# Half 1's tail into the latent attention, four masks onto POOL, ScalarE's early copies in other places of the scan

## What is computed

```python
# layer 1, first part (L1_attn): a state of 16 x 256 per batch
x_proj = x @ proj_in_w.T + proj_in_b
delta = softplus(x_proj @ B_w.T)                 # 16 step sizes per token
h = h * sigmoid(A) + x_t[:, :, None] * d_t[:, None, :]   # for t in 0..255
y_t = h.sum(axis=1) @ C_w.T + D_param * x_t
out = y @ proj_out_w.T + proj_out_b + x
# layer 1, second part (L1_xattn): 16 heads, keys and values from ctx
kv_c = kv @ W_kvc ; q_c = q @ W_dq               # 64 and 96 wide
scores = (q_nope @ k_nope.T + rope(q_rope) @ rope(k_rope).T) * scale
good = (k_ids <= qs) & (k_ids >= qs - 8)         # a window around seg_id
out = softmax(where(good, scores, -1e30)) @ v @ W_o
```

## Time and profile before

| | us |
|---|---|
| three timed runs | 761.4, 765.0, 765.1 (median 765.0) |
| profiled execution, whole | 760.8 |
| its span, first to last instruction | 759.0 |
| mean granted TensorE clock | 0.971 of full |
| busy in the span: PE, DVE, ACT, POOL | 689.7, 478.9, 319.7, 327.4 |

### The profile page before, as it was taken

One profiled execution on the slowest core, in us unless ns is written; L12 is line 12 of the kernel. 1 busy time (PEld: TensorE's weight loads), 2 busy tenths in 40 slices (PEclk: granted clock), 3 DMA queues, 4 the chain that ended last, 5 costly groups with the idle time before them and its releaser, 6 DMA issues.

```text
span 759.0 us, 12500 instructions
## 1 busy us (share of the span) xinstructions
PE 689.7 (91%) x4578; PEld 535.5 (71%) x4578; DVE 478.9 (63%) x995; ACT 319.7 (42%) x764; POOL 327.4 (43%) x475
## 2 busy tenths in 40 slices
PE   6999799999999888777999999999969999999993
PEld 5766564786576556545778777878848888888883
DVE  5488673331144589976998989872365656565656
ACT  4655533102213866533777677770132222222220
POOL 4323316310101869612866666651244445444521
PEclk9999999998999999998999999999969999999998
DMA  7000015000002000000000000003010211121001
GB/s 262 1 3 2 2 47 231 1 31 19 1 1 79 2 17 1 2 1 0 1 1 2 2 1 1 1 2 104 0 43 22 62 43 42 42 63 43 1 1 55
DMA packets 10462, 23.42 MB, mean 31 GB/s; under 512 B 2082, under 2 KB 5091, under 8 KB 10019
## 3 DMA queue, kind: packets, MB, share of 16 engines
q1 hardware_dynamic: 10402, 22.63, 9.0%
HBM read 21.58 MB, written 1.05 MB: 30 GB/s over the span
## 4 chain that ended last, share of the span: by engine, by line
PE 76%; DVE 15%; ACT 5%; issue 3%; DMA 1%; POOL 0%; POOLq 0%; DVEq 0%; SPq 0%; ACTq 0%
PE psum L399 30%; PE psum L432 8%; PE psum L934 6%; PE psum L965 4%; PE psum L651 4%; PE psum L943 3%; PE psum L455 3%; DVE A L1296 3%; DVE psum L1283 2%; PE psum L734 2%; PE psum L506 2%; PE psum L548 1%; DVE probs L1123 1%; DVE A L1190 1%; PE psum L779 1%
## 5 line engine op out<-in xcount | busy, mean ns | idle before, releaser
L399 PE MATMUL psum<-parts 128*128 128x256 f32 (+2 forms) x1440 | 254.2, 335 | 13.0 <-DVE parts L1144 7.5
L399 PEld LDWEIGHTS psum<-parts 128*128 128x128 f32 (+1 forms) x1440 | 220.5, 193 | 43.6 <-DVE parts L1144 7.5
L1764 POOL TENSOR_SCALAR probs<-probs,row_rec 128x256 f32<-128x256 f32 x128 | 60.6, 486 | 54.7 <-DVE row_rec L1134 53.9
L1474 ACT ACTIVATE probs<-probs,neg_max 128x256 f32<-128x256 f32 x128 | 64.0, 503 | 40.1 <-DVE neg_max L1127 40.1
L1714 ACT ACTIVATE A<-psum 128x512 f32<-128x512 f32 x44 | 26.3, 598 | 129.4 <-PE psum L399 129.4
L1883 POOL CAST parts<-C 128x512 fp32r<-128x512 f32 (+1 forms) x44 | 31.1, 706 | 101.9 <-PE psum L399 91.4
L1421 DVE TENSOR_TENSOR A<-A,psum 128x512 f32<-128x512 f32 x44 | 30.2, 687 | 70.1 <-PE psum L399 70.1
L934 PE MATMUL psum<-C,A 128*128 128x256 f32 x256 | 68.4, 391 | 0.0
L1884 POOL TENSOR_TENSOR parts<-C,parts 128x512 fp32r<-128x512 f32 (+1 forms) x44 | 54.9, 1248 | 3.5
L934 PEld LDWEIGHTS psum<-C,A 128*128 128x128 f32 x256 | 43.8, 190 | 15.1 <-issue 10.5
L1123 DVE TENSOR_TENSOR probs<-psum,ctxT 128x512 f32<-128x512 f32 x64 | 43.6, 681 | 15.5 <-PE psum L934 15.3
(11 more groups left out here) (215 smaller groups left out, 1243.2 us busy)
## 6 DMA issues: line engine op xcount, KB each, us to landing
C<-in_experts SPq DMA_DIRECT2D x22, 384.0 KB, 3.0
A<-in_w_o SPq DMA_DIRECT2D x1, 2048.0 KB, 12.2
x_tok<-in_x_tok SPq DMA_DIRECT2D x1, 1024.0 KB, 7.3
ctxT<-in_ctxT SPq DMA_DIRECT2D x1, 1024.0 KB, 11.0
out<-x_tok SPq DMA_DIRECT2D x8, 128.0 KB, 1.8
A<-in_w_uqT SPq DMA_DIRECT2D x1, 768.0 KB, 6.0
xT<-in_xT SPq DMA_DIRECT2D x2, 256.0 KB, 4.1
C<-in_wqk SPq DMA_DIRECT2D x1, 512.0 KB, 4.6
```

Of the source, the lines that this page charges most:

```text
L399: ins = mm(o, left[l], right[r], start=first and n == 0, stop=last and n == 2, skip_group_check=True)
L1474: last = af(slot, scores, ACT.Exp, bias=neg_max[:, u % RING[n], j:j + 1], accum_out=row_sum[:, u % RING[n], j:j + 1])
L1764: last = pool.tensor_scalar(pr, pr, row_rec[:, u % RING[n], j:j + 1], 1.0, ALU.mult, ALU.mult)
```

## The change

**Places in the scan.** ScalarE scales unit n + 1 ahead of the even copies of unit n - 1 (before: unit n). Its copies that stood at n = 1 to 9 are spread over n = 0 to 13: the two projected chunks at 0 and 1, the two token copies at 4 and 5, the key latents at 7 and 8, the latents by token at 10, the two rope products at 11 and 12, and the softplus in two parts at 12 and 13. TensorE's producers move along (step sizes 2, tokens back 3 and 4, latents 6 and 7, by token 9, ropes 10 and 11). An exponential of one column stands at n = 20 of ScalarE. The latents by token are now transposes of the copied latents, no longer products. Half 0's products, transposes and query latents come one unit earlier, its second residuals, norms and low part two half steps earlier.

**POOL.** Masks 0 to 3 are made by POOL at n = 10, 15, 16 and 26; the first rotation of keys moves from 12 to 13, the norm's root from 25 to 24. VectorE keeps masks 4 to 7.

**Queries.** `FIRST` is 4: pairs 0 to 2 are made by TensorE behind units 29 to 31, and pair 3 behind them; VectorE rotates pairs 0 and 1 behind half steps 60 and 62. The others come at steps 2(n - 4) + 4. All query latents use one bank and the rope products of the first four alternate between two.

**The tail.** The first scores wait for half step 61 only. The last state sums and outputs stand behind the scores of step 1, the last products behind those of steps 2 and 3, the transposes behind step 9, the query latents behind step 13; the parts of VectorE, ScalarE and POOL are put at like steps. `scaled` and `zT` of half 1 get other places in SBUF.

```diff
-        scaled = view(A, 8224, [P, 4, 1024]).rearrange("p r (i d) -> p r i d", i=4)
+        scaled = view(A, 12288, [P, 4, 1024]).rearrange("p r (i d) -> p r i d", i=4)
...
-        FIRST = 3
-
-        QUERIES_AT = {2 * (n - FIRST) + 1: n for n in range(FIRST, B * NPAIR)}
+        FIRST = 4
+
+        QUERIES_AT = {2 * (n - FIRST) + 4: n for n in range(FIRST, B * NPAIR)}
+        TURNS_AT, LATENTS_AT = 9, 13
...
             def latents_by_token():
...
+                    last = pe.transpose(bank[4][:, KVC * i:KVC * i + KVC], keys_b[0:KVC, i * P:(i + 1) * P],
+                                        ident[0:KVC, 0:KVC])
...
+            def query_pair(n):
...
+                if n:
+                    pe.wait_ge(sem("q_lat"), n)
+                if n >= 2:
+                    pe.wait_ge(sem("q_mul"), n if n > FIRST else n - 1)
...
-                if n == 1:
+                if n == 2:
                     step_sizes(1)
-                    tokens_back(1)
-                if n == 3:
+                if n in (3, 4):
+                    tokens_back(1, n - 3)
+                if n == 6:
...
                     key_latents(0)
-                if n == 4:
+                if n == 7:
                     key_latents(1)
-                if n == 6:
+                if n == 9:
                     latents_by_token()
-                if n == 7:
+                if n == 10:
                     key_ropes(0, 0)
-                if n == 8:
+                if n == 11:
                     key_ropes(0, 1)
...
-                if n == 22:
+                if n == 21:
                     final(3, (2, 3), out3)
-                if n == 26:
+                if n == 25:
                     ln_transposes(3, 0)
-                if n == 28:
+                if n == 27:
                     query_latents(0)
-            state_sums(7)
...
+                if n == 29:
+                    pe.wait_ge(sem("q_split"), 3)
+                    pe.wait_ge(sem("operand_lo"), QC_AT + 1)
+                if n >= 29:
+                    query_pair(n - 29)
+            query_pair(3)
+
+            def next_queries(u):
+
+                n = QUERIES_AT.get(u)
+                if u == 1:
+                    state_sums(7)
+                    outputs(1)
+                if u in (2, 3):
+                    if u == 2:
+                        pe.wait_ge(sem("q_mul"), 3)
+                    final(3, (2 * u, 2 * u + 1), out3)
+                if u == min(QUERIES_AT):
+                    pe.wait_ge(sem("ln_r"), 8 * 3 + NT)
+                if u == TURNS_AT:
+                    pe.wait_ge(sem("q_mul"), QUERIES_AT[u - 1] + 1)
+                    pe.wait_ge(sem("q_lat"), QUERIES_AT[u - 1] + 1)
+                    ln_transposes(3, 1)
+                if u == TURNS_AT + 1:
+                    pe.wait_ge(sem("ln_xT"), 4 * 3 + 4)
+                if u == LATENTS_AT:
+                    pe.wait_ge(sem("q_mul"), QUERIES_AT[u - 1] + 1)
+                    query_latents(1)
+                if u == LATENTS_AT + 1:
                     pe.wait_ge(sem("operand_lo"), QC_AT + 2)
...
+                if n is not None:
+                    query_pair(n)
...
-            query_pair(0)
-            outputs(1)
-            query_pair(1)
-            pe.wait_ge(sem("q_mul"), 1)
-            final(3, range(4, NT), out3)
-            query_pair(2)
-            pe.wait_ge(sem("q_lat"), 3)
-            ln_transposes(3, 1)
-            query_latents(1)
-            pe.wait_ge(sem("q_mul"), 3)
+            pe.wait_ge(sem("s_scan"), 2 * SCAN_UNITS - 2)
             pe.wait_ge(sem("k_add"), 4)
...
                 scan(m)
-                if m == 13:
+                if m == 26:
                     step_done(1)
...
-                if m == 45:
+                if m == 43:
                     residual3(2)
                     residual3(3)
-                if m == 49:
+                if m == 47:
                     for i in range(4):
                         normalise(3, i)
-                if m == 59:
+                if m == 57:
                     query_low(0)
...
+                if m in (60, 62):
+                    rotate_pair((m - 60) // 2)
...
             def rotate_next(u):
+
                 if u in QUERIES_AT:
                     rotate_pair(QUERIES_AT[u])
-                if u % 16 in (10, 12) and u < 16 * (B - 1):
+                if u == 1:
+                    merge(1)
+                if u in (2, 3):
+                    for i in (2 * u, 2 * u + 1):
+                        residual3(i)
+                if u == 5:
+                    for i in range(4, NT):
+                        normalise(3, i)
+                if u == LATENTS_AT:
+                    query_low(1)
+                if u % 16 in (10, 12) and 16 <= u < 16 * (B - 1):
                     window_mask(2 * (u // 16) + 2 + u % 16 // 12)
 
-            loaded(dve, "tab_qc", "tab_qs")
-            window_mask(0)
-            rotate_pair(0)
-            merge(1)
-            rotate_pair(1)
-            for i in range(4, NT):
-                residual3(i)
             rotate_pair(2)
-            for i in range(4, NT):
-                normalise(3, i)
-            window_mask(1)
-            query_low(1)
+            rotate_pair(3)
+            dve.wait_ge(sem("mask"), 4)
             attention("a4_", False, (0, 1), rotate_next)
...
+            scale_next(0)
             for n in range(SCAN_UNITS):
...
+                if n + 1 < SCAN_UNITS:
+                    scale_next(n + 1)
                 if n:
                     even_out(2 * n - 2)
                     even_out(2 * n - 1)
...
+                if n in (0, 1):
+                    projected(1, (n,))
+                if n in (4, 5):
+                    w = n - 4
+                    act.wait_ge(sem("s_xp_t"), 3 + w)
...
+                if n in (7, 8):
+                    latents_out(n - 7)
+                if n == 10:
                     act.wait_ge(sem("k_tok"), 1)
...
+                if n in (11, 12):
+                    ropes_out(0, n - 11)
+                if n in (12, 13):
+                    softplus(1, n - 12)
...
+                if n == 20:
+                    af(small[:, 0, 0:1], small[:, 1, 0:1], ACT.Exp)
+                if n == 28:
                     query_high(0)
+                if n >= 30:
+                    latent_pair(n - 30)
             even_out(2 * SCAN_UNITS - 2)
             even_out(2 * SCAN_UNITS - 1)
+            latent_pair(2)
+            latent_pair(3)
             sums_out(1)
...
+                if u == TURNS_AT:
+                    ln_out(3, 1)
+                if u == LATENTS_AT:
+                    query_high(1)
...
+            MASKS_AT = (10, 15, 16, 26)
+
+            def window_mask(i):
+
+                link(pool.tensor_scalar(distance, iota4, seg_f[:, i:i + 1], 1.0, ALU.subtract, ALU.mult))
+                link(pool.tensor_tensor(distance, distance, distance, ALU.mult))
+                pool.tensor_scalar(mask_m[:, i, :], distance, 16.0, NEG, ALU.is_gt, ALU.mult).then_inc(sem("mask"), 1)
+                pool.wait_ge(sem("mask"), i + 1)
...
-                if n == 12:
+                if n == 13:
                     loaded(pool, "tab_kc", "tab_ks")
                     rotate_keys(0)
...
-                if n == 25:
+                if n == 24:
                     rstd_of(3, (0,))
...
+                if n == 10:
+                    loaded(pool, "iota4", "seg")
+                    link(pool.tensor_copy(seg_f[:, :], seg_i[:, :]))
+                    pool.wait_ge(sem("k_tok"), 1)
+                if n in MASKS_AT:
+                    window_mask(MASKS_AT.index(n))
+                if n == 31:
+                    add_pair(0)
...
-            add_pair(0)
-            add_pair(1)
-            rstd_of(3, (1,))
-            add_pair(2)
+            for n in range(1, FIRST):
+                add_pair(n)
```

159 lines of the change are left out of this document (66 added, 93 removed).

## The result

| | us |
|---|---|
| kernel before, median of 6 runs beside the changed one | 763.34 |
| changed kernel, median of 6 runs (767.4 to 771.29) | 769.81 |
| ratio, 95% interval | 1.0086 (1.0054 to 1.0119) |
| forecast, with its range | 761.0 (753 to 769) |

What follows compares the result with a forecast made beforehand. VectorE, supplied by ScalarE, was taken to bound the scan, latencies the bridge, TensorE the attention. 7.3 - 3.4 - 1.0 + 1.0 = 3.9 us saved takes the profiled 760.8 to 756.9, the median to 761; range 753 to 769.

Steps and rivals of the forecast that it cites:

- Early copies: Scan's start: VectorE's waits for ScalarE's early copies sum to 4.5 us; c20 (VectorE's combine 20) starts at 273.5.
- Latents by token: Scan, TensorE: transposes replacing a product of 3.54 us take 0.8, between nought and 1.7.
- Masks on POOL: Scan, POOL: a mask (subtraction, square, comparison) takes 1.9 us, bounds 1.4 and 2.4.
- POOL becomes the bound: Scan's middle: POOL's rotation starts at 277.8, its queue takes 25.5 us to unit 20; c40 (VectorE's combine 40) at 304.4.
- rival of the gain eaten in the scan: Scan: masks of 2.4 and a later rope product put combine 40 3.5 us later; 764.6, no change; 15%.
- Table loads: Scan, ScalarE: split softplus costs 2.7 us; the additional load counts nothing (0 to 1.3), without the skill's drain.
- c40 to c60: Scan, VectorE's combines 40 to 60: 26.65 us of work plus 3.7 of stalls; combine 60 at 334.7.
- The stand at unit 29: Scan's end: TensorE waits for the low part, then runs the first query pair; 2.1 us, from 1.5 to 2.6.
- c60 to the first mask addition: Scan's end to attention, VectorE: combines and scans 4.0, rotations 2.6, waits 1.3, together 7.95 us; first mask addition at 342.7.
- The tail inside the attention: Attention: VectorE needs 24.4 us until TensorE's step 9 (367.1, 7.3 earlier); behind it 3.4 uncovered on TensorE.
- the four new waits: Attention: TensorE's waits at steps 9, 10, 13 and 14, put at 1.0 us together.
- the rival in which they drain the attention: Attention: none of the waits at steps 9, 10, 13, 14 covered, 8.6 us instead of 1.0; 768.7, slower; 14%.

Runs made afterwards that it cites:

- masks alone: Kernel before, with only masks 0 to 3 made by POOL at n = 10, 15, 16 and 26: 770.84 us, ratio 1.0097.
- cheap masks: Changed kernel with POOL's masks made of multiplications only, so all masks are zero: 765.88 us, ratio 1.0034.
- masks late: Changed kernel with masks 0 and 1 on POOL at n = 27 and 29, masks 2 and 3 on VectorE again: 760.17 us, ratio 0.995.
- spreading alone: Kernel before with only the new places of early work, scaling one unit further ahead and latents by token as transposes: 764.9 us, ratio 1.0024.
- all masks early, nothing spread: Changed kernel with early copies, producers, step size and first rotation back at their old places, all four masks kept on POOL: 762.88 us, ratio 1.0022.
- masks late, nothing spread: Changed kernel with POOL masks 0 and 1 at n = 27, 29, masks 2, 3 on VectorE, early work at old places: 753.96 us; again 756.29.
- the two edits alone: Kernel before with only ScalarE's scaling one unit further ahead and latents by token as transposes: 758.84 us, ratio 0.9953; again 758.77, 0.9955.
- the run of the forms: Kernel before with seven unread POOL instructions (multiply, subtract, add, compare) behind its last scaling: 759.92 us in one single run.
- the unspread kernel: The same kernel as masks late, nothing spread: 753.96 us, ratio 0.9874; again 756.29 us, ratio 0.9917.

## Why the prediction was wrong

**What one sum explains.** Two distances tell the traces apart: from c0 to POOL's first rotation, and from there to c40. Where TensorE waits for POOL, the second should be the queue's own length. Its rows in the changed kernel, without the two masks, give 27.92 - 2 x 3.11 = 21.7; add 1.64 from unit 20's scaling to c40 (309.56 to 311.20), the masks that stand there, and 1.39 where the rotation stands one unit earlier.

| kernel | c0 to rotation | rotation to c40 | queue's sum | ratio |
|---|---|---|---|---|
| before | 27.5 | 25.7 | 24.7 | 1 |
| changed | 32.7 | 29.6 | (29.6) | 1.0086 |
| masks alone | 27.7 | 30.9 | 31.0 | 1.0097 |
| cheap masks | 31.2 | 27.0 | 27.0 | 1.0034 |
| masks late | 30.2 | 23.4 | 23.3 | 0.995 |
| spreading alone | 30.0 | 23.4 | 23.3 | 1.0024 |
| all masks early, nothing spread | 25.0 | 31.0 | 31.0 | 1.0022 |
| masks late, nothing spread | 24.2 | 25.8 | 24.7 | 0.9874, 0.9917 |
| the two edits alone | 24.1 | 25.8 | 24.7 | 0.9953, 0.9955 |

With masks in the queue (masks alone, cheap masks, all masks early) the sum meets the trace within 0.1, and VectorE waits 2.7 to 3.2 ahead of c40 for transposes ahead of which TensorE had stood still for 4.6 to 5.1, until 0.1 behind POOL's scalings of unit 20; the changed kernel, with the same waits, is where the sum was read. There POOL's queue set the scan's middle. A late hand-over to POOL adds to it: without the spreading, but with all masks, the rotation begins 7.7 earlier behind c0 (25.0, 32.7).

Without masks in the queue POOL's bound is not shown. In the last two lines and in the kernel before the sum is 1 short and VectorE's own work sets c40, without a wait ahead of it. For "masks late" and "spreading alone" the sum meets the trace within 0.1 too, but c40 has no wait there either: TensorE stood 2.0 for POOL, and the copy was ready 0.3 before VectorE was. Two paths end together, POOL's queue and VectorE's waits of 4.2 between c20 and c40. So I can't put down to POOL alone the 3.5 by which the spreading alone is behind the two edits at c40 (53.4, 49.9).

Now step by step.

**Early copies: near, 1.9 short.** VectorE's waits before c20 sum to 6.1 where I had 4.5, and c20 came at 275.35, not 273.5. TensorE worked at a mean granted clock of 0.66 in 250 to 260, where I had counted with a full one; that this is the reason is not shown.

**Latents by token: right.** The transposes took 0.64 (from 272.91 to the next start at 273.55), I had 0.8.

**Masks on POOL: the step that failed first.** I priced subtraction and comparison like POOL's scaling, 0.455 each; they take 1.15 and 1.09. The upper bound, 2.4, was also too low, because all its rows were of multiplications: 3.1 each, 1.2 more. The number of inputs does not order these rows: the one-input subtraction of 1.15 is longer than the two-input square of 0.61. The Trainium skill ("GPSIMD Engine Reference", Elementwise — side-by-side cycle accounting) prices POOL's work by the element, at best some 1.8 cycles, and some 2.6 with two inputs. It gives no price for a subtraction or a comparison, and its figures give no reason for the subtraction to be the longer one; the measurement decides.

**POOL becomes the bound: right in mechanism, short in size.** The rotation began at 281.64 and not 277.8: 1.85 from TensorE's later transposes, 1.2 from mask 0, 0.8 that I can't place. The queue from there was 27.9, not 25.5: 2.4, the two masks. And c40 stood 1.64 behind unit 20, not 1.1: the eight transposes in between took 1.94 after the stand of 4.86. Together 3.8 + 2.4 + 0.6 = 6.8, which is c40 at 311.20 for my 304.4. My own rival of the gain eaten in the scan had this mechanism with 3.5; its size was wrong too, as it used the same bound of 2.4.

**Table loads: near.** The softplus's first part: a load at 281.73 of 1.28, the activation at 283.03. VectorE's wait of 2.77 ahead of c24 stands behind it, the rope product's copy and two scalings. The second part: a load at 284.64, the activation at 285.93, and a wait of 0.37 at c26. Together 3.1, where I had 2.7. The drain that the Trainium skill ("ScalarE: Activation LUTs", What ACT_TABLE_LOAD costs) adds to a load is not in this trace either: from a load's start to the activation's it is 1.29 and 1.30. The new load at 305.24 lies inside TensorE's wait for POOL and costs nothing.

**c40 to c60: 2.1 too short.** 32.4 where I had 30.35. The new wait is the one of 2.22 ahead of c42: TensorE, held by POOL at unit 20, has the first final products to make before unit 21's transposes, and no lead is left to cover them. They also take longer than in the kernel before, whose row is the first of these:

```profile
301.07 1.99 PE L816 MATMUL psum<-probsT,A 128*128 128x256 f32 x8 [0.47 <-DVE A L1308]
311.39 3.27 PE L825 MATMUL psum<-probsT,A 128*128 128x256 f32 x8
310.00:315.00 5.00, 5.00 (x21) 4.36 (x20) 2.13 (x6) 1.16 (x3) 4.91 (x7) 0.58 0.00 0
```

By that 1.3 of the 2.22 goes with the granted clock, which was down at 0.58 after TensorE had stood still for 4.86. Here the clock does cost time, as a consequence of POOL's stand; the prediction had no term for it. The wait stands wherever masks were in the queue: 2.25 with all masks early, 2.75 with the masks alone, 2.74 with cheap ones. It is not in the unspread kernel. The stand at unit 29 was 1.67 at VectorE, forecast 2.1.

**c60 to the first mask addition: 1.7 too short.** 9.7 where I had 8.0. The first eight scores ran at half clock: 3.62 for eight, against 1.89; the clock of 350 to 355:

```profile
350.00:355.00 5.00, 5.00 (x20) 3.81 (x22) 2.56 (x7) 0.76 (x2) 3.60 (x5) 0.50 0.00 0
345.00:350.00 5.00, 2.51 (x17) 2.13 (x16) 5.00 (x17) 1.79 (x5) 2.18 (x3) 0.83 0.00 0
```

TensorE had been busy for half of 345 to 350 and came to the scores at 1.2 GHz. I had allowed for this at the first query pair and forgot it at the scores.

**The tail inside the attention: 4.1 short at the front, 3.0 over behind.** From the first mask addition to TensorE at step 9 it took 28.5, not 24.4. VectorE waited 4.0 there, where I had 1.5: 2.00 for POOL's root at 371.83, 1.14 for the exponentials at 357.51, 0.67 and 0.22 for scores; of the other 1.6, 0.80 is TensorE's idle time just ahead of 381.79, and I can't place the rest. Behind step 9 the turn was cheaper: the eight transposes took 0.9, not 1.73, and of 3.4 only 0.4 shows at the end (the lag is 7.4 at step 9, 7.8 at the first product behind the attention). The rest of these 3.0 I can't place; without them the miss would have been larger. With the four new waits in these 0.4, the rival in which they drain the attention (8.6) is refuted. From c40 to that product the changed kernel takes 212.0, the one before 213.4; the seven others with the tail inside take 210.5 to 212.9, the four with neither the tail inside nor masks on POOL 212.7 to 213.7, the masks alone 216.8. I had forecast a gain of 6.3, and 1.4 came.

**The sum.** 6.8 + 2.1 + 1.7 + 4.1 - 3.0 = 11.7 too early. Forecast 3.9 earlier, so 7.8 later; the span shows 7.0. Over half of the error, 6.8, is there at c40, and 3.6 of that is one unmeasured price, taken three times. That masks over 2.5 each would bring 765 or more was said ahead, and came.

**The range.** It ended at 769, and 769.81 lies just outside. The bounds of a mask came from rows of other operations. The three unknowns of its own case were added up (3.6), but the rivals were taken one at a time, and nothing stood for what TensorE's clock does behind a stand.

**Open.** Whether the tail inside is worth anything by itself (2.5 us with overlapping intervals, two masks included); how much of the late early copies is the clock's, since between c5 and c10 it was 0.58 to 0.62 in all five kernels with the new places; and what part of the spreading's loss is POOL's where no mask is in its queue.

## What to carry to other kernels

Before you give an idle engine more work, lay out its queue from the last point at which it waited to the next point at which another engine waits for it, with every new piece in it: idle time ahead of that stretch is of no use within it. Price an operation by a row of that operation; where none exists, the bounds from other operations on the same engine must be wide, here a factor of 2.4. And spreading a supplier's copies delays whatever hangs on the last of them, and the copies stall the engine that they feed at their new places too: here 0.4 us of its waiting went from one stretch and 3.6 came into the next.

## What the runs showed of the hardware

- On POOL a subtraction or comparison over 128x256 takes 1.07 to 1.20; in the run of the forms a multiplication or addition takes 0.40 to 0.48, and a scaling in the kernel before 0.48 to 0.51. 32-bit and 16-bit output do not differ by more than 0.03.
- The scan's start, with nearly the same program ahead of it, came anywhere from 248.3 to 253.1 in fourteen traces. Distances are therefore counted from c0 throughout, and a single trace's end tells little below 5 us.
- At a granted clock of 0.50 eight scores took 3.62 and not 1.89, which cost VectorE's first step under 2 us; at 0.58 eight final products took 3.27 and not 1.99, which went into VectorE's wait. Both times TensorE had stood or been half idle just before. In 280 to 300 the masks alone had 0.97 and the changed kernel 0.59, and neither came to c40 by another time than POOL's queue gives.
